# Latent attention's inputs: one product for the shared key, its two parts summed by a matrix of ones, and another order on four engines

## The reference, cut to what matters

```python
c_q = x @ W_DQ
Qc = (c_q @ W_UQ).reshape(B, S, N_HEADS, D_H).transpose(0, 2, 1, 3)
Qr = (c_q @ W_QR).reshape(B, S, N_HEADS, D_HR).transpose(0, 2, 1, 3)
Qr = rope(Qr)
c_kv = x @ W_DKV
Kc = (c_kv @ W_UK).reshape(B, S, N_HEADS, D_H).transpose(0, 2, 1, 3)
Kr = rope((x @ W_KR)[:, None, :, :])
Kr = jnp.broadcast_to(Kr, (B, N_HEADS, S, D_HR))
V = (c_kv @ W_UV).reshape(B, S, N_HEADS, D_H).transpose(0, 2, 1, 3)
...
x = x + _L1_attn_ref(_layernorm(x, axis=-1), ...)
```

## Time and profile before

| | us |
|---|---|
| median of 3 runs | 921.68 (921.26 to 922.3) |
| the profiled execution | 920.38 |
| its span (first to last instruction) | 917.9 |
| stage `p9`, first instruction to the first of `a3` | 772.06 to 806.59 |
| PE, DVE, ACT, POOL busy over the whole span | 787.4, 575.8, 424.6, 335.0 |

### The profile page before, as it was taken

One profiled execution on the slowest core, in us unless ns is written; L12 is line 12 of the kernel. 1 busy time (PEld: TensorE's weight loads), 2 busy tenths in 40 slices (PEclk: granted clock), 3 DMA queues, 4 the chain that ended last, 5 costly groups with the idle time before them and its releaser, 6 DMA issues. The chain is left out here.

```text
span 917.9 us, 20324 instructions
## 1 busy us (share of the span) xinstructions
PE 787.4 (86%) x7484; PEld 616.4 (67%) x7484; DVE 575.8 (63%) x1417; ACT 424.6 (46%) x1242; POOL 335.0 (36%) x477
## 2 busy tenths in 40 slices
PE   5999999698999999977787399999278986967897
PEld 4788888355899999965465288888167774456334
DVE  3564656535899999977695733232577776455574
ACT  3656565563745554015365210000177884555472
POOL 2111121021899999931251261100643442133001
PEclk9899999897999999988988589999677998979899
DMA  8011710000000000000001036552545420000001
GB/s 255 18 40 52 261 30 1 2 1 1 1 1 1 1 1 2 1 1 0 1 2 48 22 116 184 172 161 69 177 133 184 108 59 2 1 2 3 0 1 46
DMA packets 42656, 49.68 MB, mean 54 GB/s; under 512 B 7008, under 2 KB 38592, under 8 KB 42304
## 3 DMA queue, kind: packets, MB, share of 16 engines
q1 hardware_dynamic: 38016, 41.32, 14.4%
q0 software_dynamic: 1536, 4.20, 1.5%
q10 hardware_dynamic: 3008, 2.88, 0.9%
HBM read 44.19 MB, written 4.19 MB: 53 GB/s over the span
## 5 line engine op out<-in xcount | busy, mean ns | idle before, releaser
L780 POOL TENSOR_TENSOR r_faded<-r_state,rec_f 128x256 f32<-128x256 f32 x128 | 82.1, 642 | 20.4 <-DVE r_state L762 9.6
L808 PE MATMUL r_u_ps<-r_t_in,l_same_head 128*128 128x256 f32 x256 | 87.7, 425 | 0.0
L786 POOL TENSOR_TENSOR r_q_in<-r_state,rec_q 128x256 f32<-128x256 f32 x128 | 82.0, 641 | 0.3 <-DVE r_state L759 0.2
L815 PEld LDWEIGHTS r_o_ps<-l_head_of,r_q_in 128*128 128x128 f32 x512 | 77.0, 191 | 6.9 <-POOL r_q_in L786 0.4
L1145 ACT ACTIVATE a_prob<-a_s_ps,a_negmax 128x256 f32<-128x256 f32 x128 | 59.1, 486 | 19.5 <-DVE a_negmax L1201 19.5
L1488 ACT ACTIVATE a_prob<-a_s_ps,a_negmax 128x256 f32<-128x256 f32 x128 | 58.6, 483 | 19.2 <-DVE a_negmax L1526 19.2
L815 PE MATMUL r_o_ps<-l_head_of,r_q_in 128*128 128x8 f32 x512 | 65.0, 236 | 0.3 <-POOL r_q_in L786 0.3
L2058 PE MATMUL m_h_ps<-m_rowsT,l_w 128*128 128x256 f32 x256 | 58.6, 389 | 0.0
L759 DVE TENSOR_TENSOR r_state<-r_update,r_faded 128x256 f32<-128x256 f32 x128 | 54.3, 424 | 4.4
L748 DVE TENSOR_TENSOR r_t_in<-r_state,r_par_ps 128x256 f32<-128x256 f32 x128 | 53.7, 420 | 5.3
L752 DVE TENSOR_TENSOR r_update<-r_u_ps,rec_k 128x256 f32<-128x256 f32 x128 | 55.2, 431 | 2.1 <-PE r_u_ps L808 2.1
(11 more groups left out here) (351 smaller groups left out, 1906.4 us busy)
## 6 DMA issues: line engine op xcount, KB each, us to landing
l_w<-in_B_w SPq DMA_DIRECT2D x16, 1024.0 KB, 6.0
a_ctxT<-in_ctxT SPq DMA_DIRECT2D x31, 256.0 KB, 2.8
a_ctx<-in_ctx SPq DMA_DIRECT2D x16, 256.0 KB, 2.7
expert_out<-m_y ACTq DMA_DIRECT2D x7, 256.0 KB, 6.0
all_X<-in_x SPq DMA_DIRECT2D x4, 256.0 KB, 5.2
l_b<-in_B_b SPq DMA_DIRECT2D x1, 1024.0 KB, 5.7
routed_rows<-ffn_xn SPq DMA_DIRECT2D x8, 128.0 KB, 1.8
l_F_up<-in_F_up SPq DMA_DIRECT2D x1, 1024.0 KB
```

The source lines that it names most:

```text
L780: nc.gpsimd.tensor_tensor(faded[m][:, :, :], state[(t + 1) % 2][m][:, :, :], row("f", t, m), ALU.mult).then_inc(faded_ready[m], 1)
L786: nc.gpsimd.tensor_tensor(q_in[t % 2][m][:, :, :], state[t % 2][m][:, :, :], row("q", t, m), ALU.mult).then_inc(q_ready[m], 1)
L808: nc.tensor.matmul(u_ps[t % 2][m][:, 0:B, :], same_head[:, :], t_in[m][:, :, :], start=False, stop=True).then_inc(u_mm[m], 1)
L815: mm = nc.tensor.matmul(o_ps[:, 2 * m + c, :, t % U], q_in[t % 2][m][:, c * (B // 2):(c + 1) * (B // 2), :], head_of[:, :], start=True, st ...
```

## The change

It touches `p9` and its weights only.

- **Shared key.** `D_KR` is half as wide: the key for half the heads, and the swapped key for the same, side by side in one product of 128 channels (`kr`). One multiplication by a table `turn` (cos above, sin below) gives both parts; a product with a 128x128 matrix `both_parts`, which has ones wherever two partitions have the same number modulo 64, sums the two parts and so spreads the sum over all heads' partitions, in a bank (`ks`). ACT places the shared key from that bank instead of from `plain_k`. POOL's addition for the key is gone.
- **Order on PE.** `kr` of both chunks, then the first pair of rotary queries and keys, the two sums `ks` with `low` of chunk 1 between them, the second such pair, and only then queries and values. What was paired as queries with keys and rotary queries with values (`channels`, `rotary_and_values`) is now rotary queries with keys and queries with values (`rotary_and_keys`, `queries_and_values`), in the same sizes.
- **Order on ACT.** Roots alternate with taken tiles; all eight tiles are taken before anything else but `low` of chunk 0; then both chunks' keys are placed; then queries and values.
- **Values.** ACT copies those of the even batches, DVE those of the odd ones; a bank is free when both have.
- **POOL** clears `mla_vals` only when all eight tiles are scaled.
- **Loads.** `D_turn` and `D_parts` come in addition, so the loads behind them move to the next batch's place.

The diff, cut to its core:

```diff
+        of_half = lambda c: [("qr", c, 0), ("k", c, 0), ("qr", c, 1), ("k", c, 1)]
+        uses = [("low", 0), ("kr", 0), ("kr", 1), ("qr", 0, 0), ("k", 0, 0), ("ks", 0), ("low", 1), ("ks", 1), ("qr", 0, 1), ("k", 0, 1), ("q", 0, 0), ("v", 0, 0), ("q", 0, 1), ("v", 0, 1)] + of_half(1) + [("q", 1, 0), ("v", 1, 0), ("q", 1, 1), ("v", 1, 1)]
+        place = {what: u for u, what in enumerate(uses)}
...
+                def shared_key(c):
+                    acc = free_bank("ks", c)
+                    pe.wait_ge(kr_taken, ONE + c + 1)
+                    nc.tensor.matmul(acc[:, :], both_parts[:, :], turned_k[c][:, :, :].rearrange("p b t -> p (b t)"), start=True, stop=True).then_inc(ks_mm, 1)
...
-                for c in range(2):
-                    pe.wait_ge(normed.taken, ONE + 4 * c + 4)
-                    from_rows(free_bank("low", c), low_w, c, low_mm)
-                    for i in range(2):
-                        from_rows(free_bank("kr", c, i), kr_w[:, :, i * P:(i + 1) * P], c, kr_mm)
-                    if c == 0:
-                        normed.turn(pe, 4)
-                        normed.turn(pe, 5)
-                    pe.wait_ge(low_ready, ONE + c + 1)
-                    for m in range(KD):
-                        channels(c, m)
-                    if c == 0:
-                        normed.turn(pe, 6)
-                        normed.turn(pe, 7)
-                    for i in range(2):
-                        rotary_and_values(c, i)
+                pe.wait_ge(normed.taken, ONE + 4)
+                from_rows(free_bank("low", 0), low_w, 0, low_mm)
+                normed.turn(pe, 4)
+                normed.turn(pe, 5)
+                from_rows(free_bank("kr", 0), kr_w, 0, kr_mm)
+                normed.turn(pe, 6)
+                normed.turn(pe, 7)
+                pe.wait_ge(low_ready, ONE + 1)
+                pe.wait_ge(normed.taken, ONE + 8)
+                from_rows(free_bank("kr", 1), kr_w, 1, kr_mm)
+                rotary_and_keys(0, 0)
+                shared_key(0)
+                from_rows(free_bank("low", 1), low_w, 1, low_mm)
+                shared_key(1)
+                rotary_and_keys(0, 1)
+                for i in range(2):
+                    queries_and_values(0, i)
+                pe.wait_ge(low_ready, ONE + 2)
+                for i in range(2):
+                    rotary_and_keys(1, i)
+                for i in range(2):
+                    queries_and_values(1, i)
...
-                def take_values(c, i):
+                def take_even_values(c, i):
                     act.wait_ge(v_mm, ONE + 2 * c + i + 1)
                     act.wait_ge(zeroed, ONE + 1)
+                    first = 8 * c + 4 * i
                     for e in range(2):
-                        for b in range(2):
-                            first = 8 * c + 4 * i + b
-                            ins = nc.scalar.activation(vblk[e * T:(e + 1) * T, first:first + 3:2, :, e * HD:(e + 1) * HD],
-                                                       bank("v", c, i)[b * T:(b + 1) * T, :].rearrange("p (t h e d) -> p t h e d", t=2, h=HH, e=2)[:, :, :, e, :], ACT.Copy)
-                    ins.then_inc(v_ready, 1)
-
-                def place_keys(c, e):
-                    act.wait_ge(kr_sum, ONE + c + 1)
-                    nc.scalar.activation(k_rope[:, c * HB:(c + 1) * HB, e, :], plain_k[c][:, :, :], ACT.Copy, scale=quad[:, e:e + 1]).then_inc(kr_ready, 1)
-
-                for g in range(NT // 2):
-                    normed.roots(act, g)
-                for t in range(4):
+                        ins = nc.scalar.activation(vblk[e * T:(e + 1) * T, first:first + 3:2, :, e * HD:(e + 1) * HD],
+                                                   bank("v", c, i)[0:T, :].rearrange("p (t h e d) -> p t h e d", t=2, h=HH, e=2)[:, :, :, e, :], ACT.Copy)
+                    ins.then_inc(v_even, 1)
+
+                def place_keys(c):
+                    act.wait_ge(ks_mm, ONE + c + 1)
+                    for e in range(4):
+                        ins = nc.scalar.activation(k_rope[:, c * HB:(c + 1) * HB, e, :], bank("ks", c)[:, :].rearrange("p (b t) -> p b t", t=T), ACT.Copy, scale=quad[:, e:e + 1])
+                    ins.then_inc(k_placed, 1)
+
+                normed.roots(act, 0)
+                normed.roots(act, 1)
+                normed.take(act, 0)
+                normed.roots(act, 2)
+                normed.take(act, 1)
+                normed.roots(act, 3)
+                normed.take(act, 2)
+                normed.take(act, 3)
+                take_low(0)
+                for t in range(4, NT):
                     normed.take(act, t)
+                place_keys(0)
+                take_low(1)
+                place_keys(1)
                 for c in range(2):
-                    take_low(c)
-                    if c == 0:
-                        normed.take(act, 4)
-                        normed.take(act, 5)
-                    for m in range(KD):
-                        take_queries(c, m)
-                    if c == 0:
-                        normed.take(act, 6)
-                        normed.take(act, 7)
                     for i in range(2):
-                        take_values(c, i)
-                    for e in range(4):
-                        place_keys(c, e)
+                        take_queries(c, i)
+                        take_even_values(c, i)
...
-                def turned(c, i, name, mm, taken, out):
-                    dve.wait_ge(mm, ONE + 2 * c + i + 1)
-                    nc.vector.tensor_tensor(out[c][:, i, :, :], bank(name, c, i)[:, :].rearrange("p (b t) -> p b t", t=T), over_positions((cos, sin)[i]), ALU.mult).then_inc(taken, 1)
+                def times_turn(c):
+                    dve.wait_ge(kr_mm, ONE + c + 1)
+                    nc.vector.tensor_tensor(turned_k[c][:, :, :], bank("kr", c)[:, :].rearrange("p (b t) -> p b t", t=T), by_head(turn), ALU.mult).then_inc(kr_taken, 1)
+
+                def take_rotary(c, i):
+                    dve.wait_ge(qr_mm, ONE + 2 * c + i + 1)
+                    nc.vector.tensor_tensor(turned_q[c][:, i, :, :], bank("qr", c, i)[:, :].rearrange("p (b t) -> p b t", t=T), by_head((cos, sin)[i]), ALU.mult).then_inc(qr_taken, 1)
...
+                def take_odd_values(c, i):
+                    dve.wait_ge(v_mm, ONE + 2 * c + i + 1)
+                    dve.wait_ge(zeroed, ONE + 1)
+                    first = 8 * c + 4 * i + 1
+                    for e in range(2):
+                        ins = nc.vector.tensor_copy(vblk[e * T:(e + 1) * T, first:first + 3:2, :, e * HD:(e + 1) * HD],
+                                                    bank("v", c, i)[T:2 * T, :].rearrange("p (t h e d) -> p t h e d", t=2, h=HH, e=2)[:, :, :, e, :])
+                    ins.then_inc(v_odd, 1)
...
-                    chunk(c)
+                    times_turn(c)
+                for c in range(2):
+                    for i in range(2):
+                        take_rotary(c, i)
+                        take_keys(c, i)
+                    for i in range(2):
+                        take_odd_values(c, i)
 
             @block.gpsimd
             def _(pool):
+                pool.wait_ge(normed.scaled, ONE + NT)
                 nc.gpsimd.memset(vblk[:, :, :, :], 0.0).then_inc(zeroed, 1)
                 for c in range(2):
-                    pool.wait_ge(kr_taken, ONE + 2 * c + 2)
-                    nc.gpsimd.tensor_tensor(plain_k[c][:, :, :], turned_k[c][:, 0, :, :], turned_k[c][:, 1, :, :], ALU.add).then_inc(kr_sum, 1)
                     pool.wait_ge(qr_taken, ONE + 2 * c + 2)
                     nc.gpsimd.tensor_tensor(q_rope[:, c * N:(c + 1) * N].rearrange("p (b t) -> p b t", t=T), turned_q[c][:, 0, :, :], turned_q[c][:, 1, :, :], ALU.add).then_inc(qr_ready, 1)
...
-    all_heads = lambda w: np.tile(w, (1, H))
+    half_heads = lambda w: np.tile(w, (1, H // 2))
...
-        "D_KR": np.concatenate([all_heads(kr), all_heads(swap(kr))], axis=1), "D_WO": f["L1_attn_W_O"],
+        "D_KR": np.concatenate([half_heads(kr), half_heads(swap(kr))], axis=1), "D_WO": f["L1_attn_W_O"],
         "D_cos": np.tile(cos, (H, 1)), "D_sin": np.tile(sin, (H, 1)),
+        "D_turn": np.concatenate([np.tile(cos, (H // 2, 1)), np.tile(sin, (H // 2, 1))]), "D_parts": (p[:, None] % R == p % R).astype(np.float32),
```

63 lines of the change are left out of this document (31 added, 32 removed).

## The result

The changed kernel takes 917.92 us (median of 7 runs, 913.87 to 919.58), the kernel before 921.68 in the same comparison: ratio 0.9950, 95% interval 0.9937 to 0.9963. Run again elsewhere (`after_again`): 917.84 against 922.78, ratio 0.9957, 0.9938 to 0.9976. The change makes the program 0.4% faster, and 917.92 is 1.0 us above the forecast.

A forecast was written before the change was run, and what follows sets the result against it. The block was taken as a chain of hand-overs with no engine full, ACT ending it. Next stage 4.4 us earlier plus 0.4 in the scores gives 4.8 off 921.7: 916.9 us, range 914.2 to 919.7.

The forecast's parts named there:

- Head: Stage's start: first scaling 0.40, first transposes 1.41 earlier, `low` starting 2.6 earlier, at 778.1.
- The clock takes some of it back: At `low`: starting earlier on half clock, it takes 3.2 instead of 2.91 and ends 2.3 earlier, at 781.3.
- as soon after its start as before: One bound for `low`: the clock rises as soon behind its start as before, so it takes 2.9.
- the late one of my two cases: Other bound for `low`: the clock rises only at 783, costing 3.43, and 0.2 more for two transposes.
- The kind clock: Rival, 18%: clock rises as early behind `low` as before and stays up into the scores; gain 6.5, 915.2.
- in the middle it did not fall: Rival, 9%: clock drops to 1.2 GHz where PE starves at the new wait; gain 2.0, 919.7.
- it did not stay down much longer than before either: Rival, slower, 4%: clock stays down from the stage's start; a rise at about 792 uses up the 4.8.
- Placements: ACT's key placements from a bank: a step of 0.55, bounds 0.49 and 0.71.
- The placements' chain and the new wait: Middle: eight placements and a `low` copy end at 793.9; PE waits about 1 us, delaying chunk 1 on DVE.
- DVE last: Block's end: DVE, from 796.0 with four value copies at 0.44 a step, ends at 801.8 to 801.9.
- Scores: Next stage's first scores: 0.4 gained of 1.7 possible if the clock stays up, bounds 0 and 1.7.
- Edits at nothing: Memset ends ten microseconds before the first value copy; added loads land before the block; neither costs time.

The follow-up runs named there:

- a_memset_first: The changed kernel with the memset of vals back at the stage's start, no longer waiting for the scaled tiles: 919.01 us, ratio 0.9960 to the kernel before.
- a_old_key: The changed kernel with the shared key made as before (two products a chunk, POOL addition, placed from SBUF), in the new order: 921.57 us, ratio 0.9992.
- b_head_fill: The kernel before plus products nobody reads (4, 2 and 1 of 128x512) in PE's idle time at the stage's start: 921.04 us, ratio 0.9995.
- b_head: The kernel before with only the memset behind the scaled tiles and roots alternating with taken tiles on ACT: 921.40 us, ratio 0.9985.
- a_values_act: The changed kernel with all value copies back on ACT, banks as changed: 920.18 us, ratio 0.9982 to the kernel before.

## Why the prediction was right, and where its sum was off

The time lies in the range and on the forecast's side, and none of the rivals happened whole. The agreement of the whole time is in part luck: in the repeat the time is 4.9 below the kernel before's, as forecast (4.8), though its stage gained only 3.2. The steps are to be judged by the stage, which gained 3.5 and 3.2 where 4.4 was forecast:

- **Head.** The first scaling took 0.39, the transposes started at 2.29 and `low` at 5.87, all as worked out. Both edits were needed: `low` starts at 8.66 with neither, at 7.24 with the memset's place alone, at 7.28 with the roots' order alone (`a_memset_first`), and at 5.87 with both.
- **The clock takes some of it back.** This step failed by its size. I took 3.2 for `low` and nothing behind it. `low` took 3.57, and behind it two transposes and the first `kr` product took 2.80 instead of 2.16. Together that is 1.0: the first placement came 17.57 behind the start, not 16.5, and what follows came 0.9 to 1.1 late, up to the stage's 31.03 instead of 30.1. The clock did not come up "as soon after its start as before". In the ten traces without fillers it came up 10.6 to 11.7 behind the stage's start, whether `low` started at 5.9, 7.2 or 8.7. Even the late one of my two cases, a rise at 783 for 3.43 and 0.2 more, was 0.6 too cheap; it left out the `kr` product altogether. The kind clock would have risen as soon behind `low` as before, and it did not; in the middle it did not fall, being 1.00 from 785.7 to 806.2; and it did not stay down much longer than before either (10.7 and 11.3, and 10.9 before). The Trainium skill says in "TensorE: Matmul & The Clock Gate", under "What's actually happening", that the point of the rise varies from run to run of the same kernel. The two traces of the changed kernel agree, with 10.7 and 11.3.
- **Placements.** I took a step of 0.55. A group of four took 2.42, which with some 0.70 for the last one is a step of 0.57. The Trainium skill's page "VectorE: DVE Perf Modes" gave an estimate of 0.57 by its section on the errata, and the trace agrees.
- **The placements' chain and the new wait.** Here the mechanism was wrong, and it cost the sum nothing. The wait was there and 0.91 long, where 1.0 was forecast. But in the forecast DVE starts chunk 1 when PE's chain behind the placements lets it, at 796.0, and I never laid DVE's own queue beside that. DVE was busy up to that point with chunk 0's second keys and odd values: these end at 799.99, and the next rotary operation starts at 800.02. So the last link into DVE's run is PE's second rotary pair of chunk 0, behind chunk 1's `low`, and not ACT's placements. `a_old_key` began the placements 0.84 earlier and gained nothing by it, and without the wait the stage stayed the same (28.62 against 28.63). The two paths reach this point at nearly the same time, and that the sum held in spite of the wrong path is luck.
- **DVE last.** It was, at 30.74 behind the start, with its copies at a step of 0.44, as taken. ACT was done 1.2 earlier.
- **Scores.** I forecast a gain of 0.4. The next stage's first shift of scores came 3.80 behind its start before, 4.86 in the first trace of the changed kernel and 3.43 in the repeat: a loss of 1.1 and a gain of 0.4. The gap in front of the scores was 2.75, and the whole of 1.6 needed it closed.
- **Edits at nothing.** The memset ended 13 us ahead of its first reader. The added loads show no cost: the repeat, which has them too, enters the stage at 771.70, and the kernel before at 772.06.

## What to carry to other kernels

When an edit starts TensorE's work earlier in a stage that begins after idle, price everything up to the point where the clock came up before at the lower level, and not only the first product. Before a new wait is charged, look at the engine that uses the waiting work: if it is busy without a hole up to that point, the wait is free. Read an effect below half a per cent from the stage in the trace, since unchanged stages moved by 3 us between two executions of one kernel here.

Then try a few products that nobody reads in PE's idle gaps. By the traces they brought 2.4 in this stage and 1.6 in the next one's first scores, where the reordering brought 3.2 to 3.5. In time the two kernels with both sets of fillers lie 9.7 and 6.2 below the kernel before, the change included, and the difference between these two is unexplained. In the old order the fillers brought 1.2 in the stage and nothing that the time shows.

## What the runs showed of the hardware

- Two 128x512 products and one of 128x256 in the idle head kept the granted clock at 1.00 for the whole stage, in three traces. In the ten traces without them the clock fell 0.4 to 1.5 behind the stage's start and read 0.50 for 10.2 to 10.3 us. Its rise came later where its fall had come later, and what PE did in between, `low` at 5.9 or at 8.7, did not move it.
- In `b_head_fill` four products of 128x512 began at the same distance from the last work (0.78), and the clock still fell, for 3.3 us. Why it fell there and not in the other three no run here tells.
- `b_head_fill` has the next stage at 0.50 for its first 11 us, and that stage is 1.3 longer than in the kernel before: in this trace what its own stage had gained is lost again (ratio 0.9995). This isn't shown to be the fillers' doing, since in `b_head` and `a_values_act`, without fillers, the clock is down as long (13.7 us, against 13.6).
- A memset on GpSimd of 3.51 costs the DVE scaling beside it 1.4 (1.81 against 0.39). The row statistics that run beside it too take as long as without it (0.75 for the first two).
